# A new order of the steps in the attention loop of a one-core Trainium2 kernel

## What is computed

```python
k = (key @ Wk.T + bk).reshape(b, lk, H, DH)
v = (value @ Wv.T + bv).reshape(b, lk, H, DH)
score = jnp.einsum('bqhd,bkhd->bhqk', q, k) / jnp.sqrt(jnp.float32(DH))
score = score + jnp.where(valid, 0.0, NEG)[:, None, :, :]
attn = jax.nn.softmax(score, axis=-1)
ctx = jnp.einsum('bhqk,bkhd->bqhd', attn, v).reshape(b, lq, d)
```

## Time and profile before

| | |
|---|---|
| median of the runs | 1582.63 us |
| the profiled execution | 1582.63 us |
| its span in the trace | 1580.8 us |
| PE busy over the span | 1389.4 us, 88% |
| DVE, ACT, POOL busy | 67%, 56%, 50% |
| body 0 to body 31 in the trace | about 92.7 to 1214.7 us |
| granted clock of PE, mean | 0.949 |

### The profile page before, as it was taken

How to read it: one execution, slowest core, us unless ns; L and a number is a source line. 1 busy time by engine, 2 the same in 40 slices (tenths; PEclk the granted TensorE clock), 3 DMA queues, 4 the chain that set the end, 5 groups by cost and what they waited for, 6 DMA issues and landing times. The chain is left out here.

```text
span 1580.8 us, 55267 instructions
## 1 busy us (share of the span) xinstructions
PE 1389.4 (88%) x24351; PEld 989.7 (63%) x24351; DVE 1061.8 (67%) x1681; ACT 881.5 (56%) x1195; POOL 789.2 (50%) x560
## 2 busy tenths in 40 slices
PE   4679999999999999999999999999997687459408
PEld 2457777777777777777777777777775355324107
DVE  7756666666666666666666666666664867785984
ACT  1445655665656565665556565656565565425742
POOL 4566555555655555555555555555530798420000
PEclk9899999999999999999999999999999898769859
DMA  4564444544444444444444444444421421010001
GB/s 150 145 137 137 107 107 110 128 120 120 117 127 132 107 107 116 121 124 122 114 136 121 107 107 120 124 124 114 117 65 53 131 54 27 1 41 0 1 0 54
DMA packets 90495, 155.97 MB, mean 99 GB/s; under 512 B 16704, under 2 KB 55496, under 8 KB 90256
## 3 DMA queue, kind: packets, MB, share of 16 engines
q1 hardware_dynamic: 88256, 150.92, 36.6%
q10 hardware_dynamic: 2000, 1.51, 0.4%
HBM read 60.95 MB, written 2.20 MB: 40 GB/s over the span
## 5 line engine op out<-in xcount | busy, mean ns | idle before, releaser
L645 DVE TENSOR_REDUCE MXP<-W_PS 128x1 f32<-128x512 f32 x768 | 510.7, 688 | 339.8 <-PE W_PS L456 338.7
L540 ACT ACTIVATE PR<-S_PS 128x1024 f32<-128x1024 f32 (+1 forms) x416 | 409.0, 1030 | 144.8 <-PE S_PS L404 142.8
L350 POOL TENSOR_TENSOR K_HI<-K,MCOL 128x512 f16<-128x512 f32 (+1 forms) x224 | 215.2, 961 | 282.8 <-ACT K L548 282.8
L356 POOL TENSOR_TENSOR CTX_LO<-CTX,CTX_HI 128x3202 f16<-128x3202 f32 x32 | 194.1, 6067 | 190.9 <-DVE CTX_HI L623 190.9
L456 PE MATMUL W_PS<-STK,QS 105*128 105x512 f16 (+1 forms) x1024 | 279.9, 336 | 10.1 <-POOL STK L377 6.1
L548 ACT ACTIVATE K<-W_PS,BK 128x512 f32<-128x512 f32 (+1 forms) x256 | 148.3, 593 | 175.9 <-PE W_PS L430 157.1
L404 PE MATMUL S_PS<-QS,STK 105*128 105x128 f16 (+1 forms) x3328 | 238.9, 220 | 4.2 <-ACT PR L540 2.9
L352 POOL TENSOR_TENSOR K_LO<-K,K_HI 128x512 f16<-128x512 f32 (+1 forms) x224 | 232.0, 1036 | 17.6
L404 PEld LDWEIGHTS S_PS<-QS,STK 105*128 105x128 f16 (+1 forms) x3328 | 210.4, 99 | 48.2 <-ACT PR L540 3.8
L439 PE MATMUL W_PS<-WV_HI,CTX_HI 128*128 128x256 f16 (+1 forms) x832 | 228.0, 274 | 2.8 <-ACT K L548 2.6
L439 PE MATMUL W_PS<-WV_HI,CTX_LO 128*128 128x256 f16 (+1 forms) x832 | 227.4, 273 | 0.0
(11 more groups left out here) (243 smaller groups left out, 1593.5 us busy)
## 6 DMA issues: line engine op xcount, KB each, us to landing
CTX<-in_ctx_t SPq DMA_DIRECT2D x64, 800.5 KB, 5.8
STK<-K_HI SPq DMA_DIRECT2D x256, 128.0 KB, 2.5
STK<-K_HI SPq DMA_DIRECT2D x256, 72.1 KB, 2.1
STK<-K_LO SPq DMA_DIRECT2D x128, 128.0 KB, 2.6
STK<-K_LO SPq DMA_DIRECT2D x128, 72.1 KB, 2.1
QSTK<-STK SPq DMA_DIRECT2D x12, 192.0 KB
SQS<-QK_HI SPq DMA_DIRECT2D x32, 64.0 KB, 2.2
X<-in_x SPq DMA_DIRECT2D x1, 1536.0 KB, 16.3
```

Source lines behind the costliest of these rows:

```text
L350: pool.tensor_tensor(K_HI[:, m, lo:hi], k32, zero, ALU.add).then_inc(k_hi, 1)
L356: pool.tensor_tensor(CTX_LO[:, u, :, :], CTX[:, :, :], CTX_HI[:, u, :, :], ALU.subtract).then_inc(ctx_lo, 1)
L540: nc.scalar.activation(PR[0:m, (NT * b + i) % PR_RING, :], S_PS[par][0:m, :], ACT.Exp).then_inc(p_sb, 1)
L645: dve.tensor_reduce(MXP[:, j, at:at + 1], bank[:, :], AX.X, ALU.max).then_inc(mx_done, 1)
```

## The change

The list `SCHEDULE` is written in another order. The same 70 steps stand in it; the functions, the buffers, the semaphores and `FIRST` stay. Two lines of the old and of the new list:

```diff
-    ("ST", 0), ("ST", 1), ("QS", 0), ("V", 0), ("MX", 0), ("ST", 2), ("OT", 0), ("ST", 3), ("V", 1), ("V", 2),
-    ("MX", 1), ("PV", 0), ("PV", 1), ("PV", 2), ("CH", 0), ("MX", 2), ("MX", 3), ("ST", 4), ("V", 3), ("MX", 4),
+    ("ST", 0), ("V", 0), ("ST", 1), ("QS", 0), ("MX", 0), ("ST", 2), ("MX", 1), ("OT", 0), ("V", 1), ("ST", 3),
+    ("V", 2), ("MX", 2), ("V", 3), ("MX", 3), ("CH", 0), ("MX", 4), ("PV", 0), ("PV", 1), ("PV", 2), ("PV", 3),
```

## The result

The changed kernel takes 1594.43 us (median of 6, 1590.38 to 1596.26) against 1582.80 (6 runs, 1582.06 to 1583.89): a ratio of 1.008, 95% interval 1.0062 to 1.0096. Forecast were 1575.7 us and a gain; measured is a loss of 11.6 us. All 28 executions of the changed kernel on record lie between 1589.35 and 1600.23 us.

A forecast was written before the change was run, and what follows sets the result against it. PE's never-waiting matmul stream was taken to bound 29 of 32 bodies. Terms -6.6 (stream), -0.5 (body 1), -0.35 (body 30) and +0.5 (body 31) sum to -6.95: from 1582.63 to 1575.7 us, range 1574.0 to 1579.2.

The forecast's parts named there:

- (1): PE's stream: runs of PV go from five to four per body, 0.22 us each, 6.6 us less; new pairs cost nothing.
- (2): PE's way from MX 3 to K 0: cover after CTX_LO's end shrinks from 1.48 to 0.4 us; costs nothing.
- Rival C: K 0 waits if CTX_LO ends 1.0 us later against the stream: 12 us lost, 7 won, 1587.6; chance 0.06.
- (3): Banks that V 1 and MX 10 take over: both are free with 0.2 us left; costs nothing.
- (4): From MT to ST 0: 2.50 us instead of 1.60; stack for the next MX 0: 7.5 instead of 6.3; costs nothing.
- (5): Body 1: the cast comes 2.6 us later, behind POOL's memset, so MX 4's wait goes: 0.5 us less.
- (6): Body 30: MT comes 0.85 us earlier, ST 0 2.1 after it: 0.35 less, between 1 less and 0.5 more.
- (7): Body 31: ST steps and ACT's exponentials shift, the last four PVs start later: 0.5 us more, between 0 and 1.5.
- D: Beside an ST or in a run of four PVs, the run's cost isn't saved: about 1582 us; chance 0.04.
- What would show it: Signs: MT to MT 0.2 us shorter with PE always busy, K 0 without wait, body 1's cast 1.8 us.

The follow-up runs named there:

- e2: The changed kernel with PV 3 moved to PV 4 and 5, PV 6 to PV 7 and 8 (runs 3, 3, 3, 4): 1607.98 us.
- e5: The changed kernel with 15 one-column matmuls ahead of each of K 1 to K 5 and 120 ahead of the loop: 1632.31 us.
- e8: The changed kernel with PV 3 moved to PV 4 to 6 and PV 9 behind PV 8 (runs 3, 4, 3, 3): 1581.86 us.
- e11: The changed kernel with PV 3 at PV 4 to 6, PV 9 and 10 at PV 7 and 8 (runs 3, 4, 4, 2): 1581.42 us.
- e1: The changed kernel with PV 9 and 10 back ahead of MX 25 (runs 4, 3, 2, 2, 2): 1589.42 us.
- e12: The changed kernel with PV 9 and 10 moved up to PV 7 and 8 (runs 4, 3, 4, 2): 1585.98 us.
- e6: The changed kernel with 15 one-column matmuls ahead of each of K 1 to K 5 and 66 ahead of the loop: 1665.37 us.

## Why the prediction was wrong

A gain of 7 us was forecast, a loss of 11.6 came. It failed at one sentence of its first part: "neither a shorter wait nor an earlier transfer can be worth anything there; the stream itself must get shorter, or a new wait must break it". The new wait came, and it is of a kind for which I had looked nowhere. I went through banks, semaphores, DVE's queue and SP's DMAs, all that the program orders. That PE's instructions themselves are transferred, 256 at a time, stood in two rows of the page (the q8 row, and the number of PE's instructions), and I gave it no term and no rival. What the runs showed in its place: PE waits at the border between two packets of its code where four PVs use one up within 2 to 3 us. The cost, by the account: 16.3 us in the middle, about 1 us in body 30 and 4.3 in body 31, against the 6.95 that the sum had as the gain.

Point by point:

- (1) Right. One run fewer is worth 0.24 us per body by the traces (0.22 forecast, with 0.20 to 0.24 as bounds). The new pairs cost nothing.
- (2) Right. The rows of POOL and PE in body 14:

```profile
614.75 6.29 POOL L356 TENSOR_TENSOR CTX_LO<-CTX,CTX_HI 128x3202 f16<-128x3202 f32 x1 [8.76 <-DVE CTX_HI L623]
```

```profile
621.42 0.60 PE L430 MATMUL W_PS<-CTX_HI,WK_HI 128*128 128x512 f16 x2
```

  CTX_LO ends at 621.04, K 0 starts 0.38 us later; forecast were 0.4. e2 took 0.45 of this cover away, and 0.2 us of waiting came in each second body. Rival C's mechanism is thus real, and it didn't act in the changed kernel.
- (3) Right: no bank wait in bodies 1 to 29.
- (4) Right: there is no wait for the stack or the row of maxima. That the longer run behind MT "grows safer" was true of that wait and wrong of the place: it is the dense stretch in which most stalls are.
- (5) Right: the cast of body 1 takes 1.82 us again (2.85 before), and MX 4 doesn't wait.

```profile
147.58 1.82 DVE L623 CAST CTX_HI<-CTX 128x3202 f16<-128x3202 f32 x1
```

- (6) Right in its mechanism: from the first MX behind V 6 to MT are 1203.15 - 1194.28 = 8.87 us (9.0 forecast, 10.5 before), and MT comes 0.93 earlier after ST 0 (0.85 forecast). From MT to MT it is 1.0 longer all the same: 0.9 are two PVs more behind the MT before it, and 1.0 PE lost at its start, at a border:

```profile
1175.58 0.19 PE L430 MATMUL W_PS<-CTX_LO,WK_HI 128*128 128x65 f16 x1 [0.87 <-issue]
```

- (7) The order itself costs what it should: in e5 body 31 takes 19.6 us from MT to its last transposes, 18.6 before, with 0.5 of it the two PVs that came behind MT (counted in (6)) and 0.5 forecast. In the changed kernel it took 23.9: a stall in the last run, and the lower clock (1.2 GHz) from 2.2 us after its end. PE's timeline there:

```profile
1206.74 0.29 PE L419 MATMUL O_PS<-PR,V 65*17 65x64 f32 x4 [1.39 <-issue]
1206.96 1.07 PE L404 MATMUL S_PS<-QS,STK 105*128 105x128 f16 x16
1208.70 0.81 PE L404 MATMUL S_PS<-QS,STK 105*128 105x128 f16 x8 [0.67 <-ACT PR L540]
1209.31 1.06 PE L469 MATMUL W_PS<-CST,OSB 128*64 128x128 f32 x4
1210.16 1.06 PE L404 MATMUL S_PS<-QS,STK 105*128 105x128 f16 x8
```

  Four transposes, 0.60 us long at the full clock, take 1.06.

Of the rivals, D came nearest by its words (in a run of four the cost isn't saved) but put 0.1 us on it and named no cause; none of them could give 1594. "What would show it" did its work: the period was shorter with no wait in it, the waits of PE listed something else, and that was the place to dig. The range, 1574.0 to 1579.2, held the unknowns of steps that I had priced, and nothing for one that I had not seen. (Its lower end is misreckoned by 0.3: 1575.7 less 2 is 1573.7.)

## What to carry to other kernels

Where an engine never waits, its own instruction stream is a transfer too: count its instructions, divide the instruction queue's bytes by its packets, and look for the stretch in which one packet's worth is used up fastest. In the changed kernel the stalls stand where 256 instructions take 2.0 to 3.2 us of undisturbed work and a border falls at their end; in the kernel before, with 4.55 us or more everywhere, there were none. The margin isn't a fixed number: in e8 a packet that started late stalled PE after a stretch of 4.9 us. Here the merged run saved 0.24 us per body, 7 us in all, and the stalls cost three times that. Before merging small matmuls, see whether large ones can stand among them, as in the 3, 4, 3, 3 and 3, 4, 4, 2 of e8 and e11. A border that stands still is another way, but the padding for it cost 50 us here.

## What the runs showed of the hardware

- Each change from full-width matmuls to the 17-column ones and back costs 0.24 us per run in this loop, whatever its length (period 35.47 us with five runs in the kernel before and 35.46 in e1, 35.23 to 35.24 with four in the changed kernel, e8, e11 and e12).
- PE's code comes in packets of 16,384 bytes that take 0.88 to 1.8 us, and PE goes on 1.2 to 1.6 us after the landing if it waits for one. The packet starts late: PE is then 50 to 283 instructions short of it (traces of before and after). At the stalls of more than 1 us in e2 and e8 it started up to 3.4 us after PE had crossed the border before.
- A one-column matmul with a 128-column weight load takes 25 ns in a row of such (0.38 us for 15).
- A stall can be followed by 3.4 us at the lower clock, but its length alone doesn't tell. In the changed kernel an idle time of 1.75 us was, and one of 1.58 wasn't; in e2 those of 1.52, 1.69 and 1.67 us were, and those of 1.86 and 1.72 weren't.
- Kernels with stalls scatter more: the 28 executions of the changed kernel lie within 10.9 us of each other, 21 of the kernel before within 5.1, four of e6 within 8.3 and four of e5 within 2.6.
